# One PSUM bank for sums and values in bursts, three for raw scores, a quarter of them in their own period

## The chip, the cores and the metric

The kernel runs on one core of a Trainium2 chip. The metric is the device time of one execution in microseconds, lower is better. The engines are TensorE (PE in the rows, with PEld for its weight loads), VectorE (DVE), ScalarE (ACT), GpSimd (POOL) and SyncE (SP), which here only issues DMAs.

## What is computed

A small transformer layer over 8 sequences of 384 tokens and 512 features. The first 256 tokens of a sequence come from a state-space convolution (einsum over V = exp(dA_log l)), the other 128 are given. Then, cut to what matters:

```python
h = concatenate([_L0_tok_ref(x, ...), txt], axis=1)
# attention: 16 query heads of 32, 4 key/value heads
scores = einsum('bhqd,bhkd->bhqk', q, k) * HD ** -0.5     # q, k rotated
attn = softmax(scores, axis=-1)
out = einsum('bhqk,bhkd->bhqd', attn, v)
h = h + einsum('bsh,oh->bso', out.reshape(b, s, H), Wo)    # x = layernorm(h) went in
# 64 experts, 6 for each token, at most 64 tokens each, and two shared ones
h = h + ffn(layernorm(h))
```

## The kernel before

The program has three stages: the state-space stage, `attention_phase` (which the change touches alone), and `experts_phase`. The instructions of each engine are written in order by hand, in one loop for each engine, and wait for counts of named semaphores; there is no scheduler. So every engine's queue is strictly in the order of the code.

`attention_phase` runs over periods b = -1 to 7. In period b the softmax and values of sequence b are made, and beside them the next sequence a = b + 1 is prepared (normalised, turned, projected, rotated, heads turned), c = b - 1 is projected out and d = b - 2 is routed to experts. A period has 16 slots n, one for each head; tables such as VALUE_STEPS, Q_SLOT, KV_SLOT and OUT_FIRST give the slot of each piece, and the same tables are read in the loops of all engines.

The pieces that the change and the prediction speak of:

- `scores(b, n)`, L853 to L862: three matmuls into banks 0 to 2, for one head. The operand QT has a row (row 96) with the negated maximum of every query, so that the exponential that follows (ScalarE, L1100) needs no subtraction. Heads 0 and 8 wait for `stacked[0]` and `stacked[1]`: the DMAs that stack the heads (`stack`, L728 and L731) and bring the maxima (`stack_max`, L737), each for half of the heads.
- `raw(a, u)`, L887 to L895, and `row_maximum(a, u)`, L1325 to L1333: unit u of 48 is one bf16 matmul of 128 queries by 384 keys, and VectorE's maximum over its row. Units 0 to 23 are heads 0 to 7, units 24 to 47 heads 8 to 15. Two banks (5 and 6) take turns, and all 48 units of the next sequence stand in slots 8 to 15, six a slot. `max_row` (L1335 to L1341) transposes the maxima of a half into `mrow`, in slots 11 and 15.
- `values(G, q)`, L864 to L885: for group G of four heads, six steps of four matmuls (each a quarter of the array's columns). Steps 0 to 2 sum the exponentials into bank 4, steps 3 to 5 multiply them with the values into bank 3. In four slots the steps are (0, 1), (2, 3), (4), (5). `invert_sums` (L1343) transposes and inverts the sums on VectorE, `divide` (L1354) multiplies.
- `turn_x` and `turn_heads` (L897, L922): transposes of the next sequence's input and of its rotated heads, in slots 0 and 7. ScalarE copies each turned head (L1206), VectorE makes its low part (`q_lo`, L1323), ScalarE converts it for the raw scores (`bf16_heads`).
- `statistics2` and `slots` on VectorE: second layer norm of d (slot 0, L1370 to L1376) and the slots of the experts (slot 1, L1418 to L1422); `routing` in slots 4 to 6 (L1382 to L1413).
- SP's order in a period: `stack(1)`, `stack_max(1)`, the rows of the next but one sequence, rows of the residual, `store_turned`, `store_rows`, `stack(0)`, `stack_max(0)`, `store_sums`.

The wait that guards the turned heads on ScalarE, in slot 7, is not touched by the change:

```python
if i == 0 and a >= 1:
    act.wait_ge(stacked[1], STACK * a)
```

STACK counts the twelve DMAs of `stack` and the four of `stack_max` of one half, so with a = b + 1 the wait is for all of `stacked[1]` up to period b.

## Time and profile before

| what | us |
|---|---|
| median of 3 runs | 1477.85 (1473.19 to 1486.64) |
| the profiled execution's own time | 1462.84 |
| its span, from the first to the last instruction | 1461.0 |
| mean granted TensorE clock | 0.947 |

The span is what the trace covers; the execution's own time is a little over it. The median of the runs is 15 us above the profiled execution. Attention runs from the first scores, at 201.51 us, and seven periods later head 0 of period 7 starts at 743.05. In rows of the trace a line such as `512.60 1.02 DVE L1294 ... x2 [1.46 <-ACT ...]` gives start, duration, engine, line, what it writes and reads, how many instructions are merged, and in brackets the idle time before it with what ended it. An fp32 matmul counts as two instructions in rows of L880.

### The profile page before, as it was taken

To read this page: it belongs to the slowest core of one execution; us is meant where nothing else is said; L and a number is where in the kernel's file an instruction comes from. 1 tells how busy PE (TensorE), PEld (TensorE's weight loads), DVE (VectorE), ACT (ScalarE), POOL (GpSimd) and SP (SyncE) were. 2 spreads that over 40 slices of the span, in tenths; PEclk is the share of its full clock that TensorE was granted. 3 is DMA by queue.
4 is the path that set the end of the run, shared out by engine and by line. 5 is a ranking of instruction groups with operands and counts; after the bars stand their busy time and mean duration, and the time that the engine had idled before them with its cause. 6 is when DMAs were issued, how large, how long until landed. Compare 5 with 4: busy or idle time off the path is not lost. (4 is left out here: it accounts for less than half of the span.)

```text
span 1461.0 us, 23472 instructions
## 1 busy us (share of the span) xinstructions
PE 1267.7 (87%) x9192; PEld 819.4 (56%) x9192; DVE 759.0 (52%) x1667; ACT 420.8 (29%) x695; POOL 501.3 (34%) x453
## 2 busy tenths in 40 slices
PE   5197578889898999989888879999999999999995
PEld 5196434344546464636444768756666656666662
DVE  6984466757676868676866352323222222232221
ACT  2211223444435354444445421111111111111110
POOL 0000101011203434343467376243444444444345
PEclk9698769999999999999999889999999999999998
DMA  3023141321505152524243384799999999998983
GB/s 114 0 60 94 30 103 41 77 50 43 142 17 146 42 131 63 128 66 107 66 137 118 118 291 74 212 309 300 330 304 302 318 337 329 282 362 290 325 267 44
DMA packets 139829, 239.82 MB, mean 164 GB/s; under 512 B 61112, under 2 KB 81224, under 8 KB 139720
## 3 DMA queue, kind: packets, MB, share of 16 engines
q1 hardware_dynamic: 115880, 214.10, 46.0%
q0 software_dynamic: 23840, 24.23, 9.2%
q8 instruction: 73, 1.20, 0.3%
q14 instruction: 36, 0.29, 0.1%
HBM read 175.59 MB, written 38.90 MB: 147 GB/s over the span
## 5 line engine op out<-in xcount | busy, mean ns | idle before, releaser
L1969 POOL DMA_INDIRECT out_rows<-mo_y,mo_scatter_half x128 | 182.1, 1423 | 244.2 <-DMA out_rows<-mo_y,mo_scatter_half 172.3
L1332 DVE TENSOR_REDUCE at_maxes<-at_ps 128x1 f32<-128x384 f32 x384 | 195.1, 551 | 63.2 <-PE at_ps L894 57.3
L1100 ACT ACTIVATE bulk<-at_ps 128x1152 f32<-128x1152 f32 x128 | 144.5, 1129 | 263.4 <-PE at_ps L861 262.3
L1592 POOL DMA_INDIRECT slot_table<-at_toki,at_si x144 | 143.3, 995 | 105.4 <-DVE at_maxes L1332 76.1
L70 PE MATMUL mo_ps<-arena_view,arena_view 128*117 128x384 f32 (+1 forms) x864 | 168.8, 344 | 1.1 <-PEq L549 1.1
L70 PEld LDWEIGHTS mo_ps<-arena_view,arena_view 128*117 128x117 f32 (+1 forms) x864 | 146.6, 179 | 14.6 <-issue 14.5
L894 PE MATMUL at_ps<-late_view,late_view 128*128 128x384 bf16 x384 | 116.7, 354 | 35.8 <-DVE at_maxes L1332 18.0
L852 PE MATMUL at_ps<-arena_view,arena_view 128*128 128x512 f32 (+1 forms) x576 | 114.8, 350 | 3.8 <-ACT arena_view L1185 2.4
L894 PEld LDWEIGHTS at_ps<-late_view,late_view 128*128 128x128 bf16 x384 | 31.2, 98 | 145.7 <-DVE at_maxes L1332 111.7
L852 PEld LDWEIGHTS at_ps<-arena_view,arena_view 128*128 128x128 f32 x576 | 90.3, 193 | 36.6 <-issue 22.3
L861 PE MATMUL at_ps<-arena_view 97*128 97x384 f32 x384 | 97.6, 363 | 9.2 <-DMA arena_view<-at_mrow 5.1
L1944 DVE SCALAR_TENSOR_TENSOR mo_hm<-mo_sil,mo_wcol,mo_ps 128x352 f32<-128x352 f32 x32 | 18.6, 580 | 155.9 <-ACT mo_sil L1868 155.9
L1564 POOL TENSOR_TENSOR arena_view<-arena_view,arena_view 128x640 f32<-128x640 f32 x24 | 37.3, 1555 | 172.4 <-DVE arena_view L1317 172.3
L852 PE MATMUL at_ps<-late_view,late_view 128*128 128x512 f32 x288 | 92.4, 437 | 4.1 <-POOL late_view L1568 2.5
L1568 POOL TENSOR_TENSOR late_view<-arena_view,late_view 128x384 fp32r<-128x384 f32 x32 | 32.0, 1012 | 171.1 <-ACT late_view L1164 171.1
L485 PE MATMUL ss_psK<-arena_view,bulk 64*64 64x64 f32 x2048 | 61.5, 221 | 30.8 <-DVE bulk L431 30.8
L880 PE MATMUL at_ps<-bulk,at_ones 128*32 128x384 f32 x768 | 86.1, 528 | 0.5 <-DVE at_maxes L1332 0.5
L1814 PE MATMUL mo_ps<-bulk,mo_xgT 128*64 128x352 f32 x512 | 81.0, 470 | 5.0 <-DVE mo_xgT L1937 5.0
L880 PE MATMUL at_ps<-bulk,arena_view 128*32 128x384 f32 x768 | 83.3, 508 | 0.0
L78 PE MATMUL mo_ps<-arena_view,arena_view 117*128 117x512 f32 (+1 forms) x324 | 78.9, 397 | 4.9 <-DVE arena_view L1901 4.9
L861 PEld LDWEIGHTS at_ps<-arena_view 97*128 97x128 f32 x384 | 68.5, 195 | 25.5 <-ACT bulk L1100 8.2
L1814 PE MATMUL mo_ps<-late_view,mo_xgT 128*64 128x352 f32 x512 | 79.3, 462 | 1.7 <-DVE mo_xgT L1937 1.7
(218 smaller groups left out, 1820.5 us busy)
## 6 DMA issues: line engine op xcount, KB each, us to landing
bulk<-in_L_ffn_w_gate SPq DMA_DIRECT2D x32, 704.0 KB, 7.4
bulk<-in_L_ffn_w_up SPq DMA_DIRECT2D x32, 704.0 KB, 8.9
late_view<-in_L_ffn_w_gate SPq DMA_DIRECT2D x32, 704.0 KB, 7.5
late_view<-in_L_ffn_w_up SPq DMA_DIRECT2D x32, 704.0 KB, 9.2
arena_view<-arena_view SPq DMA_DIRECT2D x96, 192.0 KB
late_view<-in_L_ffn_w_down SPq DMA_DIRECT2D x32, 512.0 KB, 6.1
bulk<-in_L_ffn_w_down SPq DMA_DIRECT2D x32, 512.0 KB, 6.4
out_rows<-at_hr SPq DMA_DIRECT2D x8, 768.0 KB, 3.8
```

The source lines that it names most:

```text
L70: m = T.matmul(out, self.gu[:, wa, g, k, self.SO[c]:self.SO[c] + self.SW[c]], self.x2[:, xa, k, :], start=(n == 0), stop=(n == last))
L78: m = T.matmul(out, self.h[0:self.SW[c], xa, c, s * P:(s + 1) * P], self.d[0:self.SW[c], wa, c, :], start=(n == 0), stop=(n == last))
L485: m = T.matmul(psK[half, n % 2, i * STEP:(i + 1) * STEP], Pm[half, k % 2, t, h, :], basis, start=(t == 0), stop=(t == 3))
L852: m = T.matmul(out, xs[:, xa, k, x_cols], ws[:, wa, k, w_cols], start=(n == 0), stop=(n == 3 * KC - 1))
L861: m = T.matmul(ps[:, kt, 0:SEQ], QT[:, NH + h // REP, kt * P:(kt + 1) * P], QT[:, h, :], start=True, stop=True)
L880: m = T.matmul(ps[HD * j:HD * (j + 1), 3 + sums, 0:SEQ], w, PT[:, (REP * G + j) % RING, kt, :], start=(kt == 0), stop=(kt == NT - 1))
L894: T.matmul(ps[:, raw_bank(a, u), 0:SEQ], qb[:, r, s * P:(s + 1) * P], kb[:, g, :], start=True, stop=True).then_inc(raw_scores, 1)
L1100: A.activation(PT[:, N % RING, :, :], ps[:, 0:NT, 0:SEQ], ACT.Exp, scale=float(HD) ** -0.5)\
L1332: V.tensor_reduce(maxes[:, half, s, h:h + 1], ps[:, raw_bank(a, u), 0:SEQ], AX.X, ALU.max, negate=True)\
L1592: G.indirect_dma_start(slot_table, bass.IndirectOffsetOnAxis(ap=si[:, e % 2, m:m + 1], axis=0), toki[:, e % 2, m // TOPK:m // TOPK + 1], N ...
L1814: m = M.matmul(ps[CAP * e:CAP * (e + 1), 1 + g, 0:I], xgT[:, k, CAP * e:CAP * (e + 1)], wgu[j][:, e, g, k, :], start=(k == 0), stop=(k == ...
L1969: G.indirect_dma_start(acc_halves, bass.IndirectOffsetOnAxis(ap=scatter_half[:, half, 2 * p + e:2 * p + e + 1], axis=0), y[:, p % 2, e, co ...
```

## The change

Sums and values of a group now share bank 3. All three steps of the sums stand in the first slot of a group, all three of the values in the third. `invert_sums` moves to the second slot, `divide` to the fourth, and the values wait for the first transpose of the inversion, which reads the sums out of the bank. Bank 4 is free for raw scores: units 0 to 35 of the next sequence (36 units, four or five a slot) rotate over banks 4, 5 and 6 and wait for the maximum three units back; units 36 to 47 are made in their own sequence's period, in slots 0 to 6, all in bank 4, each waiting for the maximum of the unit before. Sequence 0 keeps its old places. `max_row` of the second half moves from slot 15 of the period before to slot 6 of the own one, that of the first half from slot 11 to 13. On SP `stack_max(1)` moves behind `store_turned`, and in the last period the first load of shared rows behind it. GpSimd's scatters wait for maxima scaled to 36.

```diff
-        VALUE_STEPS = {0: (0, 1), 1: (2, 3), 2: (4,), 3: (5,)}
+        VALUE_STEPS = {0: (0, 1, 2), 1: (), 2: (3, 4, 5), 3: ()}
...
+        AHEAD_UNITS = 36
+        RAW_EARLY = {1: 37, 2: 39, 4: 42, 5: 44, 6: 46}
+        RAW_LATE = {0: 36, 1: 38, 2: 40, 3: 41, 4: 43, 5: 45, 6: 47}
+
         def raw_units(b, n):
...
-            if -1 <= b < B - 1 and n >= RAW_FROM and (b >= 0 or n < RAW_FROM + REP):
-                return b + 1, range(PER_SLOT * (n - RAW_FROM), PER_SLOT * (n - RAW_FROM + 1))
+            if b == -1 and RAW_FROM <= n < RAW_FROM + REP:
+                return 0, range(PER_SLOT * (n - RAW_FROM), PER_SLOT * (n - RAW_FROM + 1))
+            if 0 <= b < B - 1 and n >= RAW_FROM:
+                return b + 1, range(AHEAD_UNITS * (n - RAW_FROM) // (NH - RAW_FROM),
+                                    AHEAD_UNITS * (n - RAW_FROM + 1) // (NH - RAW_FROM))
             return b + 1, ()
 
+        def own_units(b, n, when):
+            return (when[n],) if b >= 1 and n in when else ()
+
         def raw_bank(a, u):
-            return (7, 4)[u % 2] if a == 0 and u >= HALF_UNITS else 5 + u % 2
+            if a == 0 and u >= HALF_UNITS:
+                return (7, 4)[u % 2]
+            return 4 + u % 3 if u < AHEAD_UNITS else 4
...
-                    if b > 0:
-                        sp.wait_ge(mrow_ready, 2 * b + 2)
-                        stack_max(1)
...
                     store_turned(d)
+                if b > 0:
+                    sp.wait_ge(mrow_ready, 2 * b + 2)
+                    stack_max(1)
+                if b == B - 1:
+                    for done in stacked:
+                        sp.wait_ge(done, STACK * B)
+                    sp.wait_ge(x2T_stored, 16 * (B - 3))
+                    shared_rows_in(0)
+                if prev2:
                     store_rows(d)
...
                 if q == 0:
                     pe.wait_ge(probs_ready, REP * (G + 1))
-                    wait(pe, divide_step, DIVIDE_STEPS * (G - 1) + 1 if G else 0)
-                    wait(pe, max_ready, 0 if G else UNITS)
+                    wait(pe, o_ready, G)
                 if q == NT:
                     pe.wait_ge(v_copied, NT * (b + 1))
-                    wait(pe, o_ready, G)
+                    pe.wait_ge(divide_step, DIVIDE_STEPS * G + 1)
...
-                wait(pe, max_ready, UNITS * a + u - 1)
+                if u < AHEAD_UNITS and (a > 0 or u < HALF_UNITS):
+                    wait(pe, max_ready, UNITS * a + max(u - 2, 0))
+                else:
+                    wait(pe, max_ready, UNITS * a + (u if a else u - 1))
...
-                    for q in steps[0:1]:
+                    for q in steps:
                         values(G, q)
+                    for u in own_units(b, n, RAW_EARLY):
+                        raw(b, u)
                     if prev2 and n == 4:
                         logits(d)
...
+                    for u in own_units(b, n, RAW_LATE):
+                        raw(b, u)
                     for u in units[4:]:
                         raw(of, u)
...
-                    if n % REP == 0:
-                        divide(NKV * b + n // REP - 2)
+                    if n % REP == 1:
+                        invert_sums(NKV * b + n // REP - 1)
+                    if n % REP == REP - 1:
+                        divide(NKV * b + n // REP - 1)
...
+                    for u in own_units(b, n, RAW_EARLY):
+                        row_maximum(b, u)
                     if prev2:
                         routing(d, n)
                     for u in units[2:4]:
                         row_maximum(of, u)
-                    if n % REP == REP - 2:
-                        invert_sums(NKV * b + n // REP - 1)
+                    for u in own_units(b, n, RAW_LATE):
+                        row_maximum(b, u)
...
-                    if nxt and n in (NH * 3 // 4 - 1, NH - 1) and (a > 0 or n < NH - 1):
-                        max_row(a, (n - RAW_FROM) // REP)
-                    if b == 0 and n == REP - 1:
-                        max_row(0, 1)
+                    if nxt and n == (RAW_FROM + REP - 1 if a == 0 else RAW_FROM + 5):
+                        max_row(a, 0)
+                    if main and n == (REP - 1 if b == 0 else 6):
+                        max_row(b, 1)
```

TensorE at the start of period 4, before. L861 are scores, L904 the turns of the next input (late_view_54 is the identity), L880 the sums (from at_ones) and values, L852 projections, 128x512 for queries and 128x256 for keys and values:

```order
L904 MATMUL at_ps<-late_view_54,arena_view_1714 128x128 x6
L880 MATMUL at_ps<-bulk,at_ones 32x384 x4
L904 MATMUL at_ps<-late_view_54,arena_view_1714 128x128 x6
L880 MATMUL at_ps<-bulk,at_ones 32x384 x4
L861 MATMUL at_ps<-arena_view_1724 128x384 x3
L880 MATMUL at_ps<-bulk,at_ones 32x384 x4
L880 MATMUL at_ps<-bulk,arena_view_1723 32x384 x4
L852 MATMUL at_ps<-arena_view_65,arena_view_1715 128x512 x12
L861 MATMUL at_ps<-arena_view_1724 128x384 x3
L880 MATMUL at_ps<-bulk,arena_view_1723 32x384 x4
L852 MATMUL at_ps<-arena_view_65,arena_view_1715 128x256 x12
```

And after, where the same lines are L875, L920, L893 and L866, and L910 is a raw score:

```order
L920 MATMUL at_ps<-late_view_54,arena_view_1714 128x128 x6
L893 MATMUL at_ps<-bulk,at_ones 32x384 x12
L920 MATMUL at_ps<-late_view_54,arena_view_1714 128x128 x6
L910 MATMUL at_ps<-late_view_1722,late_view_1721 128x384
L875 MATMUL at_ps<-arena_view_1724 128x384 x3
L910 MATMUL at_ps<-late_view_1722,late_view_1721 128x384
L866 MATMUL at_ps<-arena_view_65,arena_view_1715 128x512 x12
L910 MATMUL at_ps<-late_view_1722,late_view_1721 128x384
L875 MATMUL at_ps<-arena_view_1724 128x384 x3
L893 MATMUL at_ps<-bulk,arena_view_1723 32x384 x12
L910 MATMUL at_ps<-late_view_1722,late_view_1721 128x384
L866 MATMUL at_ps<-arena_view_65,arena_view_1715 128x256 x12
```

The sums are one burst between the turns, the values one burst in slot 2, and a raw score of the own sequence stands on either side of the first projection.

VectorE in the same place, before: L1294 makes the low parts of the input, L1365 adds the residual, L1370 to L1376 are the second statistics, L1418 to L1422 the slots of the experts:

```order
L1294 TENSOR_TENSOR arena_view_1715<-at_ps,arena_view_1715 128x384 x4
L1365 TENSOR_TENSOR at_hr<-at_hr,at_ps 128x512
L1370 BN_STATS at_bn<-at_hr 128x6 x3
L1373 BN_AGGR at_mv<-at_bn 128x2 x3
L1375 TENSOR_SCALAR at_shift<-at_mv 128x3
L1376 TENSOR_SCALAR at_ve<-at_mv 128x3
L1418 TENSOR_REDUCE at_sf<-at_hv 128x18
L1420 CAST at_si<-at_sf 128x18
L1421 CAST at_toki<-at_tokf 128x3
L1422 TENSOR_SCALAR at_tokf<-at_tokf 128x3
```

After, with L1350 a row maximum and L1367 to L1369 the inversion of the sums:

```order
L1312 TENSOR_TENSOR arena_view_1715<-at_ps,arena_view_1715 128x384 x4
L1383 TENSOR_TENSOR at_hr<-at_hr,at_ps 128x512
L1388 BN_STATS at_bn<-at_hr 128x6 x3
L1391 BN_AGGR at_mv<-at_bn 128x2 x3
L1393 TENSOR_SCALAR at_shift<-at_mv 128x3
L1394 TENSOR_SCALAR at_ve<-at_mv 128x3
L1350 TENSOR_REDUCE at_maxes<-at_ps 128x1
L1367 STREAM_TRANSPOSE arena_view_1725<-at_ps 128x384
L1368 RECIPROCAL at_rcol<-arena_view_1725 128x12
L1369 STREAM_TRANSPOSE arena_view_1725<-at_rcol 128x384
L1436 TENSOR_REDUCE at_sf<-at_hv 128x18
```

The maximum of unit 36 stands behind the second statistics, and the inversion between it and the expert slots; two more maxima follow those.

VectorE in slots 6 and 7 of period 4, before: L1403 to L1413 are the routing, L1323 the low parts of the heads, L1332 the first maxima of the next sequence:

```order
L1403 RECIPROCAL at_rsum<-at_ssum 128x3
L1405 TENSOR_SCALAR late_view_1727<-late_view_1728,at_rsum 128x64 x3
L1411 TENSOR_TENSOR late_view_1728<-at_ps,at_base 128x192
L1412 TENSOR_SCALAR at_lg<-late_view_1728 128x192
L1413 TENSOR_TENSOR at_base<-at_base,at_ps 128x64
L1349 STREAM_TRANSPOSE arena_view_1725<-at_ps 128x384
L1350 RECIPROCAL at_rcol<-arena_view_1725 128x12
L1351 STREAM_TRANSPOSE arena_view_1725<-at_rcol 128x384
L1323 TENSOR_TENSOR arena_view_1720<-at_ps,arena_view_1719 128x384 x5
L1332 TENSOR_REDUCE at_maxes<-at_ps 128x1 x2
```

And after:

```order
L1350 TENSOR_REDUCE at_maxes<-at_ps 128x1
L1421 RECIPROCAL at_rsum<-at_ssum 128x3
L1423 TENSOR_SCALAR late_view_1727<-late_view_1728,at_rsum 128x64 x3
L1429 TENSOR_TENSOR late_view_1728<-at_ps,at_base 128x192
L1430 TENSOR_SCALAR at_lg<-late_view_1728 128x192
L1431 TENSOR_TENSOR at_base<-at_base,at_ps 128x64
L1350 TENSOR_REDUCE at_maxes<-at_ps 128x1
L1358 STREAM_TRANSPOSE at_mrow<-at_maxes 128x96
L1377 TENSOR_TENSOR arena_view_1726<-at_ps,arena_view_1725 128x384
L1341 TENSOR_TENSOR arena_view_1720<-at_ps,arena_view_1719 128x384 x5
L1350 TENSOR_REDUCE at_maxes<-at_ps 128x1 x6
```

A maximum stands before the routing and one behind it, the transpose of the maxima (L1358) follows, then a division in place of the inversion, and then the low parts.

## Rows read from the trace of the kernel before

**Rows 1.** Stretches: length, busy us (count) of PE, PEld, DVE, ACT, POOL; clock, DMA share
```profile
201.51:278.75 77.24, 64.33 (x364) 33.59 (x364) 53.10 (x119) 28.46 (x39) 5.68 (x5) 0.90 0.26 57
...
510.27:552.60 42.33, 38.06 (x269) 25.30 (x267) 29.75 (x82) 23.50 (x44) 15.41 (x17) 0.96 0.49 131
552.60:587.85 35.25, 33.21 (x201) 15.50 (x202) 28.93 (x59) 11.96 (x14) 16.71 (x18) 1.00 0.21 44
...
743.05:771.72 28.67, 21.75 (x167) 10.80 (x165) 16.19 (x46) 17.36 (x29) 19.66 (x21) 0.91 0.79 236
```

**Rows 2.** Groups by line, 552.60 to 587.85: busy us, mean ns, idle before
```profile
L1332 DVE TENSOR_REDUCE at_maxes<-at_ps 128x1 f32<-128x384 f32 x48 | 24.4, 551 | 6.3 <-PE at_ps L894 4.7 <-issue 1.3
...
L894 PE MATMUL at_ps<-late_view,late_view 128*128 128x384 bf16 x48 | 13.6, 333 | 2.5 <-DVE at_maxes L1332 1.4 <-issue 0.5
L852 PE MATMUL at_ps<-late_view,late_view 128*128 128x512 f32 x36 | 11.8, 437 | 0.0
```

**Rows 3.** Timeline of TensorE, period 4, and two steps of sums in period 7
```profile
510.27 0.69 PE L861 MATMUL at_ps<-arena_view 97*128 97x384 f32 x3
...
514.94 0.79 PE L861 MATMUL at_ps<-arena_view 97*128 97x384 f32 x3
...
517.09 3.06 PE L852 MATMUL at_ps<-arena_view,arena_view 128*128 128x512 f32 x12
519.99 0.69 PE L861 MATMUL at_ps<-arena_view 97*128 97x384 f32 x3
...
526.27 0.77 PE L861 MATMUL at_ps<-arena_view 97*128 97x384 f32 x3
...
530.32 0.77 PE L861 MATMUL at_ps<-arena_view 97*128 97x384 f32 x3
...
538.26 0.69 PE L861 MATMUL at_ps<-arena_view 97*128 97x384 f32 x3
...
541.83 0.69 PE L861 MATMUL at_ps<-arena_view 97*128 97x384 f32 x3
...
544.44 0.77 PE L861 MATMUL at_ps<-arena_view 97*128 97x384 f32 x3
...
552.60 0.48 PE L894 MATMUL at_ps<-late_view,late_view 128*128 128x384 bf16 x2 [0.51 <-issue]
...
743.67 1.50 PE L880 MATMUL at_ps<-bulk,at_ones 128*32 128x384 f32 x16
745.10 0.79 PE L861 MATMUL at_ps<-arena_view 97*128 97x384 f32 x3
```

**Rows 4.** Timeline of VectorE, first half of period 4
```profile
515.97 1.88 DVE L1370 BATCH_NORM_STATS2 at_bn<-at_hr 128x6 f32<-128x512 f32 x3
...
518.38 1.34 DVE L1418 TENSOR_REDUCE at_sf<-at_hv 128x18 f32<-128x1152 f32 x1
...
522.50 0.57 DVE L1349 STREAM_TRANSPOSE arena_view<-at_ps 128x384 f32<-128x384 f32 x1
...
534.25 1.88 DVE L1282 BATCH_NORM_STATS2 at_bn<-arena_view 128x6 f32<-128x512 f32 x3 [5.20 <-DMA arena_view<-in_txt]
...
541.06 1.97 DVE L1391 TENSOR_TENSOR at_hot<-at_iota,at_mf 128x384 bf16<-128x384 f32 x3
...
547.30 0.21 DVE L1413 TENSOR_TENSOR at_base<-at_base,at_ps 128x64 f32<-128x64 f32 x1
```

**Rows 5.** Timeline of ScalarE, slot 7 of period 4: first and last copies of turned heads
```profile
546.91 0.87 ACT L1206 ACTIVATE arena_view<-at_ps 128x384 fp32r<-128x384 f32 x2 [0.47 <-PE at_ps L931]
...
551.41 0.49 ACT L1206 ACTIVATE arena_view<-at_ps 128x384 fp32r<-128x384 f32 x1
```

**Rows 6.** Timeline of all engines ahead of period 0: a row of maxima on its way
```profile
197.03 0.28 DVE L1340 STREAM_TRANSPOSE at_mrow<-at_maxes 128x96 f32<-128x96 f32 x1
197.34 3.01 SPq L737 DMA_DIRECT2D arena_view<-at_mrow  x4
...
201.51 1.33 PE L861 MATMUL at_ps<-arena_view 97*128 97x384 f32 x3 [5.11 <-DMA arena_view<-at_mrow]
```

20 lines of the change are left out of this document (7 added, 13 removed).

## The prediction

> **What bounds the kernel now.** The page tells that TensorE and VectorE are both well filled while attention runs, but not which of them sets the pace, so I read the stretches by stage next. In the first half of period 4 (from the scores of head 0, at 510.27, to the first raw score of the next sequence, at 552.60: 42.33 us) TensorE is busy for 38.06 us and VectorE for 29.75; in the second half (35.25 us) they are busy for 33.21 and 28.93 [rows 1]. Then the groups of the second half: VectorE spends 24.4 us on the 48 row maxima and idles 6.3 before them, mostly for the raw scores; TensorE idles 2.5 before the raw matmuls [rows 2]. So the second half is a ping-pong over two banks in which either engine is nearly full. The first half, read in the timelines, is one chain through both engines [rows 3, 4], and it ends with the turned heads: ScalarE copies five of them, VectorE makes the low parts, and only then can the first raw score start [rows 5]. Neither half has much room, so what is added to a chain is likely to show.
>
> **The change, part by part.** Times from here on count from 510.27, in period 4; slot n is the work around head n.
>
> Second half. 36 of the 48 raw scores stay, over three banks. VectorE loses 12 maxima of 0.51 us each (24.4 / 48): 6.1 us. TensorE: two steps of sums in succession take 1.43 us (743.67 to 745.10) [rows 3], so a burst of three is 2.1 and four bursts are 8.4. The eight scores are about 0.55 each, 4.4; the 36 raw scores about 0.2 each, 7.2; the output projection keeps its 36 matmuls, 11.8 us of busy time [rows 2], of which some 10 count beside the overlap of one with the next. That is 30.0. In slots 9, 11 and 13 VectorE (five maxima and an inversion of 1.4 us, or a division and a residual) has 1.0 to 1.3 us more to do than TensorE, and three banks hide only a part. I take 2.3 us of waits: 32.3, against 35.25, a gain of 3 a period. Its ends are 0 (the bursts win nothing) and 6.1 (all the maxima removed count).
>
> First half, slots 0 and 1. Now scores 1 start at 4.67 and the first query projection at 6.82 [rows 3]. With three steps of sums between the turned inputs, scores 1 start near 4.5. But the maximum of unit 36, issued in slot 0, stands on VectorE behind the second statistics, which run from 5.70 to 8.1 [rows 4], and 0.4 later in the new order: it ends at 9.0. Unit 37 writes the same bank 4 and waits for it, and the projection stands behind unit 37: it starts at 9.3 and ends at 12.2. Unit 38 waits for maximum 37, which stands behind the inversion (1.45 us, from 12.23 now) and the slot sums (2.85 us, from 8.11 now) [rows 4]: 9.0 + 1.45 + 2.85 + 0.5 = 13.8. So scores 2 start at 14.2, where they start at 9.72 now.
>
> Slots 2 to 7, by how long each lasts now between scores [rows 3]. Slot 2: 6.28, plus 1.3 (a burst for one step) and 0.4 (two raw scores): 7.95, scores 3 at 22.1. Slot 3: 4.05; a step of values goes, but it covered a wait for the copied values, so 4.2, scores 4 at 26.3. Slot 4: 7.94, plus 0.7 (three steps for two) and two raw scores, 8.8: scores 5 at 35.1. Slot 5: 3.57, minus two steps, plus two raw scores, plus 1.6 for maximum 44, which stands behind inversion and rope (together 2.7): scores 6 at 39.2. Slot 6: 2.61, plus 1.3, plus the wait of unit 46 for maximum 45, behind the one-hot work (3.0 us, from 30.8 now [rows 4]): scores 7 at 43.7. VectorE then has the routing of slot 6 (3.0 us, ending at 37.2 now), maximum 47 and the transpose of the maxima. The row of maxima is ready at 47.3.
>
> The landing. Four small DMAs carry that row into the operand of the scores. They are issued in slot 2 now, long before scores 8 want them. At the one place where the scores wait for such DMAs, the transpose ends at 197.31, the four issues take 3.01 us and the scores start at 201.51, 4.2 us later [rows 6]. So the row lands at 51.5. ScalarE's first copy of a turned head (L1206) has a wait for stacked[1] that counts all periods so far, and it now waits for exactly this landing. From that copy to the first raw score are 5.69 us (546.91 to 552.60) [rows 3, 5], nearly all of it ScalarE's own work; I take 5.5. First raw score at 57.0, against 42.33: +14.7. With the second half's -3, a full period is 11.7 longer. The Trainium skill ("DMA: Bandwidth & Descriptors", section Rules for kernel authors) says to issue a DMA early and wait for it late, so that its fixed cost is overlapped, and the change does the opposite. This trace agrees, with the 1.2 us from the end of the last issue to the scores [rows 6].
>
> Bounds of the first half. If every new wait in slots 1, 5 and 6 were covered, the 12 raw scores (2.4) and the landing behind a row ready at about 40 would be left: near +7. If each wait is a third longer than I have it, +18.
>
> Other edits. No exponential, projection or scatter is added. GpSimd's scatter thresholds follow the 36 units; its queue waits for the maxima, not they for it. The next rows are issued 2.9 us earlier on SP, which takes away VectorE's wait of 5.20 before the statistics at 23.98 [rows 4]; in the chain above the statistics start at 27.0, so this wins nothing more. The shared bank 3 lets values wait for the first transpose of the inversion, issued a slot earlier: nothing, or 0.8 once at the end of the stage.
>
> **The sum.** Periods 3 to 5: 3 x 11.7 = 35. Period 6: 12. Period 2 has no slot sums, so unit 38 waits less: 10.5. Period 1 has neither second statistics nor routing; its row of maxima is ready at 36.5 by the same steps, and the landing makes it +9.4 - 3 = 6.4. Period 0 (77.24 us [rows 1]) keeps its first half, and in its second VectorE loses the 6.1 with little else to do: -6.5. The fill before it has three banks: -1. Period 7 has short slots, and its scores 8 start 28.67 after its head 0 now [rows 1]; stalls and landing put them near 40, and I take +10. Together 35 + 12 + 10.5 + 6.4 - 6.5 - 1 + 10 = 66.4. The profiled execution took 1462.84 by its own time, so 1529; the median of the runs shown, 1477.85, is 15 us above that execution, and I set the sum on it: 1544, say 1545.
>
> **Rivals.** First, the kernel gains. In the second half the ping-pong over two banks is what bounds, and the 6.1 us of maxima removed count in full, 43 us over seven periods, while the twelve moved ones fall into VectorE's idle time of the first half (42.33 - 29.75 = 12.6 us [rows 1]). For it: that idle time is twice what they need. Against it: queues run in order, and the second statistics lie just between two units of one bank. It decides at the row of maxima: ready by 37 after the period's start, it lands before ScalarE asks; later than that it delays. With half of the 43 kept it gives -20, 1458.
>
> Second, only the landing counts. Units 37, 38, 44 and 46 wait less than I found, the first half grows by 8, and the second shrinks by 4: 6 x 4 + 10 - 6.5 - 1 = 26.5, 1504. For it: TensorE idles 4.3 us of the first half now, and new waits may lie in the old ones' place.
>
> Third, the clock on top. It is granted at 0.96 in the first half of period 4 and at 1.00 in the second; in period 7's short slots, where TensorE is busy 21.75 of 28.67 us, it is 0.91 [rows 1]. With waits of 4 us in slot 1 and 7 around slot 8, a mean lower by 0.03 to 0.05 over a first half of 57 us would cost 1.7 to 2.9 us, 12 to 20 over seven periods: 1557 to 1565. "TensorE: Matmul & The Clock Gate" of the Trainium skill (section Why this matters for your kernels) warns of idle gaps between bursts of matmuls; by that rule my error would lie on this side.
>
> **How the numbers follow.** The chain as worked out gets 0.60, the landing alone 0.15, the clock on top 0.15, the gain 0.10, part of which ends near zero. A change of 1% is about what a measurement of this kernel can tell from none. So faster by over 1% gets 0.07, within 1% 0.07, slower by over 1% 0.86. The range goes from 1500 (the landing alone, a little less) to 1572 (the clock, with waits somewhat longer than I have them). The likeliest case alone would be 1525 to 1562.
>
> **What would show it.** Right: ScalarE's copy of the first turned head idle until the landing of DMAs from at_mrow in periods 1 to 6; TensorE waiting about 4 us in slot 1 for a row maximum; first halves of 55 to 59 us and second halves of 30 to 34. Wrong: first halves under 46 us, the row of maxima ready within 40 us of the period's start, or second halves still of 35. A granted clock under 0.92 in the first halves would speak for the third rival.

## The result

The changed kernel took 1559.13 us (median of 4 runs, 1553.81 to 1566.12), the kernel before beside it on the same chip 1477.16 (4 runs, 1473.19 to 1486.64). The ratio is 1.0548, with a 95% interval of [1.0482, 1.0613]: slower by 82 us. The forecast was 1545, slower by 67, in a range of 1500 to 1572.

The profiled execution of the changed kernel took 1566.12, 7 above its median, that of the kernel before 1462.84, 14 below its own. So the two traces lie 103 us apart, not 82. Up to head 15 of period 7 the difference is 88 (starts at 883.2 and 795.1). The other 15 us lie behind it, where the change moves only one thing, the first load of shared rows; that load was not tested by itself. The same stretch takes 662 to 683 us in the traces of all the kernels below (666 before, 681 changed), so I read nothing from it.

First the stretches of the changed kernel, in the columns of [rows 1]: the first half of period 4 (534.35 is its head 0), the second half, and period 7 up to head 8.

```profile
534.35:591.23 56.88, 41.24 (x280) 28.97 (x279) 33.70 (x95) 23.71 (x44) 16.26 (x18) 0.87 0.36 98
591.23:626.92 35.69, 32.24 (x189) 16.66 (x190) 21.90 (x47) 11.49 (x14) 15.82 (x17) 0.91 0.21 44
...
811.02:858.20 47.18, 27.84 (x178) 14.26 (x176) 24.63 (x63) 18.23 (x29) 26.98 (x28) 0.73 0.48 144
```

The first half grew by 14.6 us (42.33 before), while TensorE is busy only 3.2 more: most of it is waits. The second half did not shrink (35.25 before) though VectorE has 7 us less to do in it. Period 7 needs 47.18 to reach head 8, where it took 28.67. The granted clock fell in all three, from 0.96, 1.00 and 0.91 to 0.87, 0.91 and 0.73.

The groups of the second half, columns as in [rows 2], now with 36 units:

```profile
L1350 DVE TENSOR_REDUCE at_maxes<-at_ps 128x1 f32<-128x384 f32 x36 | 17.8, 550 | 13.8 <-PE at_ps L910 7.9 <-remote 5.8
...
L910 PE MATMUL at_ps<-late_view,late_view 128*128 128x384 bf16 x36 | 11.2, 354 | 4.6 <-issue 1.8 <-DVE at_maxes L1350 1.8
L866 PE MATMUL at_ps<-late_view,late_view 128*128 128x512 f32 x36 | 11.2, 441 | 0.7 <-DVE at_hr L1383 0.7
```

What VectorE gained by twelve maxima (24.4 to 17.8) went into idle time before the others (6.3 to 13.8), mostly for raw scores. TensorE idles more too, 4.6 for 2.5. Neither is the one that is full.

### The profile page after: what moved, and what is told of

Read it like the earlier page. It is cut to its first block and busy times, and to the rows that moved or that the text cites. A ratio compares the mean times of both kernels' runs of the same rounds, so it can differ in the third digit from the quotient of the medians.

```text
span 1564.3 us, 23475 instructions
## 1 busy us (share of the span) xinstructions
PE 1280.9 (82%) x9192; PEld 855.4 (55%) x9192; DVE 740.7 (47%) x1667; ACT 420.4 (27%) x695; POOL 501.4 (32%) x453
## 5 line engine op out<-in xcount | busy, mean ns | idle before, releaser
L1350 DVE TENSOR_REDUCE at_maxes<-at_ps 128x1 f32<-128x384 f32 x384 | 195.2, 551 | 184.7 <-PE at_ps L910 166.9
L910 PE MATMUL at_ps<-late_view,late_view 128*128 128x384 bf16 x384 | 124.0, 363 | 84.0 <-DVE at_maxes L1350 60.2
L70 PEld LDWEIGHTS mo_ps<-arena_view,arena_view 128*117 128x117 f32 (+1 forms) x864 | 146.5, 179 | 14.6 <-issue 14.5
L910 PEld LDWEIGHTS at_ps<-late_view,late_view 128*128 128x128 bf16 x384 | 33.7, 100 | 183.4 <-DVE at_maxes L1350 107.7
L866 PE MATMUL at_ps<-arena_view,arena_view 128*128 128x512 f32 (+1 forms) x576 | 125.5, 372 | 9.3 <-ACT arena_view L1203 7.8
L875 PE MATMUL at_ps<-arena_view 97*128 97x384 f32 x384 | 108.3, 394 | 12.7 <-DMA arena_view<-at_mrow 11.4
L866 PEld LDWEIGHTS at_ps<-arena_view,arena_view 128*128 128x128 f32 x576 | 98.6, 206 | 26.2 <-DVE arena_view L1335 9.8
L866 PE MATMUL at_ps<-late_view,late_view 128*128 128x512 f32 x288 | 85.1, 428 | 9.5 <-DVE at_hr L1383 4.9
L875 PEld LDWEIGHTS at_ps<-arena_view 97*128 97x128 f32 x384 | 75.6, 210 | 21.1 <-DMA arena_view<-at_mrow 12.1
L893 PE MATMUL at_ps<-bulk,at_ones 128*32 128x384 f32 x768 | 84.2, 581 | 0.3 <-ACT bulk L1118 0.3
L485 PEld LDWEIGHTS ss_psK<-arena_view,bulk 64*64 64x64 f32 x2048 | 62.4, 139 | 32.5 <-issue 32.5
```

The lines of the kernel that those rows point to most:

```text
L70: m = T.matmul(out, self.gu[:, wa, g, k, self.SO[c]:self.SO[c] + self.SW[c]], self.x2[:, xa, k, :], start=(n == 0), stop=(n == last))
L485: m = T.matmul(psK[half, n % 2, i * STEP:(i + 1) * STEP], Pm[half, k % 2, t, h, :], basis, start=(t == 0), stop=(t == 3))
L866: m = T.matmul(out, xs[:, xa, k, x_cols], ws[:, wa, k, w_cols], start=(n == 0), stop=(n == 3 * KC - 1))
L875: m = T.matmul(ps[:, kt, 0:SEQ], QT[:, NH + h // REP, kt * P:(kt + 1) * P], QT[:, h, :], start=True, stop=True)
L893: m = T.matmul(ps[HD * j:HD * (j + 1), 3, 0:SEQ], w, PT[:, (REP * G + j) % RING, kt, :], start=(kt == 0), stop=(kt == NT - 1))
L910: T.matmul(ps[:, raw_bank(a, u), 0:SEQ], qb[:, r, s * P:(s + 1) * P], kb[:, g, :], start=True, stop=True).then_inc(raw_scores, 1)
```

## The chain of waits in the trace

TensorE in slots 0 to 2 of period 4, and then around head 8:

```profile
534.36 0.69 PE L875 MATMUL at_ps<-arena_view 97*128 97x384 f32 x3
...
538.63 0.82 PE L875 MATMUL at_ps<-arena_view 97*128 97x384 f32 x3
543.67 0.50 PE L910 MATMUL at_ps<-late_view,late_view 128*128 128x384 bf16 x1 [4.21 <-DVE at_maxes L1350]
543.76 5.52 PE L866 MATMUL at_ps<-arena_view,arena_view 128*128 128x512 f32 x12
549.09 0.54 PE L910 MATMUL at_ps<-late_view,late_view 128*128 128x384 bf16 x1
549.18 1.07 PE L875 MATMUL at_ps<-arena_view 97*128 97x384 f32 x3
...
591.23 0.80 PE L910 MATMUL at_ps<-late_view,late_view 128*128 128x384 bf16 x2 [1.82 <-issue]
591.96 3.16 PE L893 MATMUL at_ps<-bulk,at_ones 128*32 128x384 f32 x24
...
600.12 2.14 PE L893 MATMUL at_ps<-bulk,arena_view 128*32 128x384 f32 x24
```

VectorE at the same start:

```profile
540.65 1.88 DVE L1388 BATCH_NORM_STATS2 at_bn<-at_hr 128x6 f32<-128x512 f32 x3
...
543.06 0.55 DVE L1350 TENSOR_REDUCE at_maxes<-at_ps 128x1 f32<-128x384 f32 x1
...
545.01 1.35 DVE L1436 TENSOR_REDUCE at_sf<-at_hv 128x18 f32<-128x1152 f32 x1
...
546.99 0.56 DVE L1350 TENSOR_REDUCE at_maxes<-at_ps 128x1 f32<-128x384 f32 x1
```

Unit 36 was made before 538.63, but its maximum stands behind the second statistics and starts at 543.06. So unit 37 waits 4.21 us for it, and the query projection with it. Maximum 37 stands in the same way behind inversion and expert slots (546.99). But it is done at 547.55, and unit 38 starts at 549.09: what holds unit 38 is the projection, which runs at half clock and takes 5.52 us.

The row of maxima at the end of the first half, on SP and on ScalarE:

```profile
581.61 2.96 SPq L748 DMA_DIRECT2D arena_view<-at_mrow  x4
```

```profile
585.77 0.87 ACT L1224 ACTIVATE arena_view<-at_ps 128x384 fp32r<-128x384 f32 x2 [5.49 <-DMA arena_view<-at_mrow]
```

ScalarE had nothing else to do and waited 5.49 us, until 4.16 after the first issue. In [rows 5] the same copy starts without such a wait. ScalarE waits six times for these DMAs in the whole trace, 30.7 us together, once in each of periods 1 to 6; it doesn't wait for them at all in the kernel before. What TensorE waited for in the first half of period 4 (us in all, times, longest) are these two above all, the maxima and, at 586.91, the turned heads behind the landing:

```profile
PE at_ps L910 <- DVE at_maxes L1350: 6.3, 4, 4.2
PE at_ps L947 <- DVE arena_view L1341: 5.7, 1, 5.7
```

## The experiments

Each kernel was made from the kernel before or from the changed one. The ratio is to the kernel before as it ran beside each of them; its median there was 1474 to 1483, so the ratios compare a little better than the medians. Beside the ratio, the table gives the means of periods 3 to 5 in the profiled execution, in us: first half (head 0 to the first raw score of the next sequence), second half, time at half clock (1.2 GHz), and, for period 7, head 0 to head 8. A profiled execution can lie 14 us from its median, so differences below 2 us a period are not to be read alone.

| kernel | median | ratio to before | first | second | half clock | to head 8, period 7 |
|---|---|---|---|---|---|---|
| before | 1477.16 | 1 | 42.4 | 36.1 | 4.6 | 28.7 |
| changed | 1559.13 | 1.0548 | 56.7 | 35.3 | 20.5 | 47.2 |
| e1, bursts, shared bank, 3 raw banks | 1515.34 | 1.0254 | 45.4 | 39.0 | 10.2 | 30.2 |
| e2, the same with 2 raw banks | 1536.60 | 1.0411 | 44.7 | 43.0 | 10.2 | 34.2 |
| e10, bursts alone | 1530.29 | 1.0391 | 44.6 | 42.2 | 13.7 | 28.2 |
| e3, changed, landing split off | 1531.36 | 1.0358 | 51.5 | 34.5 | 12.5 | 48.6 |
| e4, changed, maxima 36, 37 first | 1531.60 | 1.0356 | 53.2 | 34.8 | 12.5 | 44.6 |
| e5, changed, added matmuls | 1543.87 | 1.0483 | 56.5 | 33.3 | 8.0 | 47.6 |
| e9, e3 to e5 together | 1494.62 | 1.0144 | 50.6 | 31.7 | 0 | 40.2 |
| e6, e1 with added matmuls | 1497.90 | 1.0163 | 44.4 | 37.7 | 1.1 | 34.2 |
| e7, before with added matmuls | 1473.78 | 0.9959 | 42.7 | 35.3 | 2.3 | 29.1 |
| e8, spread steps, shared bank, 3 raw banks | 1495.62 | 1.0136 | 46.3 | 35.8 | 6.8 | 35.2 |
| e11, e8 with early inversion | 1474.28 | 0.9985 | 45.6 | 36.4 | 8.0 | 28.3 |
| e12, e11 with added matmuls | 1474.79 | 0.9951 | 44.5 | 35.2 | 0 | 34.2 |

### e1 and e2: the bursts and the banks without the moved units

Both are the kernel before with this (cut to the main lines), all 48 raw scores staying ahead:

```diff
-VALUE_STEPS = {0: (0, 1), 1: (2, 3), 2: (4,), 3: (5,)}
+VALUE_STEPS = {0: (0, 1, 2), 1: (), 2: (3, 4, 5), 3: ()}
...
-ps[HD * j:HD * (j + 1), 3 + sums, 0:SEQ]
+ps[HD * j:HD * (j + 1), 3, 0:SEQ]
...
                 if q == NT:
                     pe.wait_ge(v_copied, NT * (b + 1))
-                    wait(pe, o_ready, G)
+                    pe.wait_ge(divide_step, DIVIDE_STEPS * G + 1)
...
-                    if n % REP == 0:
-                        divide(NKV * b + n // REP - 2)
+                    if n % REP == 1:
+                        invert_sums(NKV * b + n // REP - 1)
+                    if n % REP == REP - 1:
+                        divide(NKV * b + n // REP - 1)
```

e1 has besides:

```diff
-            return (7, 4)[u % 2] if a == 0 and u >= HALF_UNITS else 5 + u % 2
+            return (7, 4)[u % 2] if a == 0 and u >= HALF_UNITS else 4 + u % 3
```

and each raw score of it waits for the maximum three units back instead of two.

> The kernel before with the bursts, the shared bank 3 and raw scores over three banks, but all 48 raw scores ahead, as before. If the moved raw scores and the late landing of the maxima are the whole of the loss, this is no slower than before: 2 to 3 us a period are won in the second half (33 to 34 us from the first raw score instead of 35 to 37) and the inversion out of slot 6 takes about 1 us off the first half, 1455 to 1468 against a median of 1477. If the bursts themselves cost (values and sums in one bank, each waiting for VectorE), it is 1490 or more.

> The kernel before with the bursts and the shared bank 3 alone; the raw scores keep two banks. If the third bank is what helps the second half, this lies 12 to 20 us above the one with three banks, at 1472 to 1485, since slots without values now have four to six raw scores in succession over two banks. If the bursts help by themselves, it lies within 5 us of the one with three banks.

Measured: e1 1515.34, ratio 1.0254 [1.0173, 1.0335]; e2 1536.60, 1.0411 [1.0338, 1.0485]. So this half of the change, which I had as a help, costs 40 us by itself, and 61 without the third raw bank. The third bank is worth 21, all of it in the second half (43.0 to 39.0). That is about half of the 82, and it was in none of my cases. Costs that are measured alone need not add up in the changed kernel, though: there the second half has only 36 raw scores.

### e10: the bursts alone

e2 with the banks of the kernel before:

```diff
-ps[HD * j:HD * (j + 1), 3, 0:SEQ]
+ps[HD * j:HD * (j + 1), 3 + sums, 0:SEQ]
...
                 if q == NT:
                     pe.wait_ge(v_copied, NT * (b + 1))
-                    pe.wait_ge(divide_step, DIVIDE_STEPS * G + 1)
+                    wait(pe, o_ready, G)
```

> The kernel before with the bursts alone: all sums of a group in its first slot into bank 4, all values in its third into bank 3, inversion in the second slot and division in the fourth, two raw banks and all 48 units ahead. It differs from the kernel with bursts, shared bank and two raw banks (1536.6, +61 over before) in the sharing only. If it is the sharing (sums wait for the division, values for the inversion) that costs, this runs at 1480 to 1500. If it is the bursts (twelve matmuls in one slot, none in the next), it stays at 1520 to 1540.

Measured: 1530.29, 1.0391 [1.0327, 1.0456], the same as e2 within the intervals. It is the bursts; with them the shared bank costs nothing that can be told. What they do is in the trace. TensorE of e10 at the start of the second half of period 4:

```profile
584.24 0.80 PE L894 MATMUL at_ps<-late_view,late_view 128*128 128x384 bf16 x2 [1.12 <-issue]
584.97 4.07 PE L880 MATMUL at_ps<-bulk,at_ones 128*32 128x384 f32 x24
588.97 0.51 PE L894 MATMUL at_ps<-late_view,late_view 128*128 128x384 bf16 x2
589.97 0.80 PE L894 MATMUL at_ps<-late_view,late_view 128*128 128x384 bf16 x2 [0.49 <-DVE at_maxes L1330]
...
592.13 0.80 PE L894 MATMUL at_ps<-late_view,late_view 128*128 128x384 bf16 x2 [0.37 <-DVE at_maxes L1330]
...
594.55 0.80 PE L894 MATMUL at_ps<-late_view,late_view 128*128 128x384 bf16 x2 [0.82 <-DVE at_maxes L1330]
```

and VectorE beside it:

```profile
584.75 1.02 DVE L1330 TENSOR_REDUCE at_maxes<-at_ps 128x1 f32<-128x384 f32 x2 [0.61 <-PE at_ps L894]
589.35 3.18 DVE L1330 TENSOR_REDUCE at_maxes<-at_ps 128x1 f32<-128x384 f32 x6 [3.57 <-PE at_ps L894]
```

Two raw scores fill the two banks, then the burst runs for 4.07 us, and VectorE is through with both maxima after 1.02 and idles 3.57. Behind the burst the raw scores come without anything between them, and TensorE waits for maxima, three times in this piece. In the kernel before one step (0.85 us) stands between two pairs of raw scores, about as long as the two maxima need. Over the second half the groups of e10 read:

```profile
L1330 DVE TENSOR_REDUCE at_maxes<-at_ps 128x1 f32<-128x384 f32 x48 | 24.4, 553 | 13.9 <-PE at_ps L894 13.5
...
L894 PE MATMUL at_ps<-late_view,late_view 128*128 128x384 bf16 x48 | 15.0, 350 | 7.8 <-DVE at_maxes L1330 5.3 <-issue 1.1
```

VectorE idles 7.6 more than in [rows 2] and TensorE 5.3 more, with the same work: both wait in turn. A part is the clock: this burst ran at half of it, and a full period has 13.7 us of half clock for 4.6. How much of the 56 us that is was not tested in this kernel; e6 below tests it in e1.

### e3: the landing split off

The changed kernel, with semaphores of their own for the maxima, on which the scores wait but ScalarE's head copy does not:

```diff
-... mrow[HD * j:HD * j + NH // 2, half, :, :]).then_inc(stacked[half], 16)
+... mrow[HD * j:HD * j + NH // 2, half, :, :]).then_inc(maxed[half], 16)
...
                     pe.wait_ge(stacked[2 * h // NH], STACK * (b + 1))
+                    pe.wait_ge(maxed[2 * h // NH], MAXED * (b + 1))
```

`max_row` on VectorE also waits for the earlier `maxed` only, no longer for the stacked heads.

> The changed kernel, with the four DMAs of the maxima on semaphores of their own, so that ScalarE's copy of the turned heads waits for the stacked heads alone and only the scores wait for the maxima. My theory: the copies start near 46 us of a full period instead of 51.4, scores 8 still wait for the landing at 51.4, and the first raw score comes near 52 instead of 56.9. Six periods of 4 to 5 us: about 28 us less than the changed kernel, near 1531. The rival, that the granted clock carries the loss behind slot 8: under 10 us less, with the same half-clock time of 20 us a period.

Measured: 1531.36, 1.0358 [1.0287, 1.0429], 28 less than the changed kernel. ScalarE starts the copies of period 4 at once (head 0 stands at 520.0):

```profile
564.35 1.13 ACT L1122 ACTIVATE bulk<-at_ps 128x1152 f32<-128x1152 f32 x1 [1.17 <-PE at_ps L879]
565.38 0.87 ACT L1228 ACTIVATE arena_view<-at_ps 128x384 fp32r<-128x384 f32 x2
...
572.37 1.13 ACT L1122 ACTIVATE bulk<-at_ps 128x1152 f32<-128x1152 f32 x1 [2.33 <-PE at_ps L879]
```

That is 45.4 after head 0, where the changed kernel had 51.4. The second half shrank a little too, with less half clock (12.5 for 20.5), so a part of the 28 is clock. Period 7, where no head is turned, gained nothing: 48.6 to head 8, for 47.2.

### e4: maxima 36 and 37 first

The changed kernel, on VectorE alone (the two maxima go from their old places in slots 0 and 1):

```diff
+                    if b >= 1 and n == 0:
+                        row_maximum(b, RAW_LATE[0])
+                        row_maximum(b, RAW_EARLY[1])
                     if prev2 and n == 0:
                         residual(d, NT - 1)
                         statistics2(d)
```

> The changed kernel, with the maxima of units 36 and 37 ahead of the residual and the second statistics on VectorE. My theory of queue order: unit 37 and the query projection behind it no longer wait for the statistics, scores 2 come near 9 to 10 us of a period instead of 14.8, unit 39 then waits some 2 us for maximum 38 behind the expert slots, scores 3 come near 19.2 instead of 22.9, and the row of maxima 3 to 4 us earlier: about 20 us less than the changed kernel, near 1538. If the row of maxima is bound by VectorE's work in slots 4 to 6 rather than by this wait, scores 3 move and the landing doesn't: within 5 us of the changed kernel.

Measured: 1531.60, 1.0356 [1.0265, 1.0447], also 28 less. TensorE, with head 0 at 527.3:

```profile
533.52 0.34 PE L910 MATMUL at_ps<-late_view,late_view 128*128 128x384 bf16 x1 [1.09 <-DVE at_maxes L1350]
533.62 3.01 PE L866 MATMUL at_ps<-arena_view,arena_view 128*128 128x512 f32 x12
...
536.51 0.82 PE L875 MATMUL at_ps<-arena_view 97*128 97x384 f32 x3
538.21 2.14 PE L893 MATMUL at_ps<-bulk,arena_view 128*32 128x384 f32 x24 [0.88 <-DVE arena_view L1367]
541.57 0.34 PE L910 MATMUL at_ps<-late_view,late_view 128*128 128x384 bf16 x1 [1.22 <-DVE at_maxes L1350]
```

The wait of 4.21 is 1.09 now, and the projection behind it takes 3.01 instead of 5.52. Scores 2 start 5.6 earlier, at 9.2 after head 0, but two new waits stand in slot 2: the values for the inversion (0.88) and unit 39 for maximum 38 (1.22). Of the 5.6, the first half kept 3.5. Here too a part is clock: 2.5 us of the 5.6 are the projection, which no longer runs at half clock behind the long wait.

### e5, e6 and e7: the clock

All three add matmuls whose result is not read, into a bank that is free there, where TensorE waits in slots 6 to 8: 30 a period in the changed kernel (e5), 18 in e1 (e6), 6 in the kernel before (e7). e5's core (two more stand in slot 6):

```diff
+            def fill(bank, count):
+                for _ in range(count):
+                    T.matmul(ps[:, bank, :], WxT[:, 0, 0, 0:P], WxT[:, 0, 0, 0:512], start=True, stop=True)
...
+                    if main and nxt and n == 8:
+                        fill(4, 6)
...
+                    if main and nxt and n == 7:
+                        pe.wait_ge(probs_ready, NH * b + 8)
+                        fill(0, 22)
```

> The changed kernel with 30 more fp32r matmuls of 512 columns a period, whose results nobody reads, placed where TensorE waits anyway: 2 before the places in slot 6, 22 before the last two turned heads in slot 7 (TensorE idles 5.7 us there), 6 behind scores 8. They show what the low clock costs, since no wait is taken away. If the clock falls because TensorE waits for the landing, the half-clock time of a full period goes from 20 us to 10 or less, slot 8 from 7.2 us to about 5.5, and the kernel is 10 to 20 us faster than the changed one although it computes more. If the clock doesn't matter, it is unchanged or up to 8 us slower.

> Bursts and three banks with all 48 raw scores ahead, plus 18 such idle matmuls a period: 10 before the places in slot 6 (2.5 us of waiting there), 2 in slot 7, 6 behind scores 8. Theory: with the values out of slots 5 and 7, TensorE has nothing to do while VectorE makes the mask and the low parts, its clock falls, and the first burst then takes 3.9 us instead of 2.1. So half-clock time should go from 10 us a period to under 4, slot 8 from 8.2 to 5 to 6, and the time to 1490 to 1500. The rival, that the bursts cost by the order of the raw scores and their maxima: the half-clock time falls, but the kernel stays at 1510 or above.

> The kernel before with 6 idle matmuls a period in slots 6 and 7. It has 3.4 us of half clock a period, of which the raw scores of slot 8 pay a part: up to 1.5 us a period, so 1466 to 1477 against 1476. No change if its clock falls for other reasons.

Measured: e5 1543.87, 1.0483 [1.0400, 1.0566]; e6 1497.90, 1.0163 [1.0098, 1.0228]; e7 1473.78 (10 runs), 0.9959 [0.9917, 1.0001]. By the medians that is 15 us in the changed kernel and 17 in e1, by the ratios 10 and 13, and in the traces head 15 of period 7 comes 9 and 13 us earlier. The intervals of each pair overlap, so the size is not sharp: 10 to 15 us and 13 to 17 are the clock. In the kernel before it is nothing that can be told. e5's stretches of period 4, head 0 at 529.10:

```profile
529.10:585.70 56.60, 46.82 (x310) 33.13 (x309) 33.69 (x95) 23.69 (x44) 16.28 (x18) 0.94 0.36 98
585.70:618.70 33.00, 29.32 (x189) 15.73 (x190) 21.85 (x46) 11.52 (x14) 15.76 (x17) 1.00 0.22 47
```

The first half is as long as in the changed kernel, since the half clock in slot 1, behind the long wait, is still there (the added matmuls stand later). The second half runs at 2.4 GHz throughout (1.00) and is 2.7 shorter. The first burst in it takes 2.14 us instead of 3.16:

```profile
586.14 2.14 PE L897 MATMUL at_ps<-bulk,at_ones 128*32 128x384 f32 x24
```

The Trainium skill ("TensorE: Matmul & The Clock Gate", section HAM oscillation) counts the penalty as half of the throttled time. By that rule, as an estimate, the 81 us less at half clock over the whole trace (281 in the changed kernel, 200 in e5) would be 40 us. The run shows 10 to 15. A likely reason, not tested, is that much of that time TensorE was waiting anyway.

### e9: the three cures together

The edits of e3, e4 and e5 in one kernel.

> The changed kernel with a semaphore of its own for the landing of the maxima, with maxima 36 and 37 ahead of the second statistics, and with 30 matmuls a period whose result is not read in the waits around slots 6 to 8. Alone these gave -28, -28 and -15 us. If they cure three different waits, most of it adds up: 1485 to 1500. If ScalarE's head copy, once freed from the landing, waits for the last maxima or the scores of head 8 instead, or if the matmuls only help where a wait is long, the cures overlap and it stays at 1505 to 1520. The bursts with the shared bank, which alone cost 38 us over the kernel before, stay in; by either theory it stays slower than before.

Measured: 1494.62, 1.0144 [1.0097, 1.0191]. The three alone gave 28, 28 and 15, together 71 (by the ratios 28, 28 and 10, together 66); here 64.5 are gone (60 by the ratio). So they are in the main three different losses; in the main only, because e3 and e4 had each taken some half clock away too. What e9 still has over the kernel before, at full clock, is in its stretches of period 4:

```profile
516.60:567.20 50.60, 43.85 (x310) 31.64 (x308) 33.50 (x95) 23.94 (x45) 15.99 (x18) 1.00 0.41 110
567.20:598.90 31.70, 28.70 (x190) 15.52 (x190) 22.05 (x46) 11.29 (x14) 16.09 (x17) 1.00 0.22 49
```

In the means, bursts and moved quarter together cost 8.2 in the first half (50.6 against 42.4) and bring 4.4 in the second (31.7 against 36.1). In the first half of period 4 TensorE still waits four times for maxima, 3.9 us in all.

### e8, e11 and e12: the shared bank without bursts

e8 is e1 with the steps spread over the four slots of a group again, but in the shared bank; inversion and division stay in the second and fourth slot, at their ends:

```diff
-VALUE_STEPS = {0: (0, 1, 2), 1: (), 2: (3, 4, 5), 3: ()}
+VALUE_STEPS = {0: (0, 1), 1: (2,), 2: (3, 4), 3: (5,)}
```

> Shared bank 3 and three banks for all 48 raw scores, as in the run with bursts, but the steps spread again: (0, 1), (2), (3, 4), (5) in the four slots of a group, with the inversion at the end of the second slot and the division at the end of the fourth. If it is the bursts and the gaps they leave that cost, this has the first half of before (40 to 42 us), a second half of 33 to 35 and about 3.4 us of half clock a period: 1455 to 1480. If it is the shared bank itself, with its wait of the values for the inversion, it stays at 1500 or above.

Measured: 1495.62, 1.0136 [1.0055, 1.0217]: 20 less than e1, but 16 over the kernel before, in between the two expectations. Its second half is that of the kernel before (35.8), so the bursts' part is gone. In the first, slot 2 takes 10.5 us where it took 6.3:

```profile
513.99 0.69 PE L861 MATMUL at_ps<-arena_view 97*128 97x384 f32 x3
516.61 2.13 PE L879 MATMUL at_ps<-bulk,arena_view 128*32 128x384 f32 x16 [1.94 <-DVE arena_view L1351]
518.67 2.61 PE L852 MATMUL at_ps<-arena_view,arena_view 128*128 128x256 f32 x12
```

The values wait 1.94 for the inversion to read the sums out of the bank, and what follows runs partly at half clock. That inversion (L1351) stood on VectorE behind the expert slots. e11 moves it ahead of them, and in the other groups ahead of the third raw maximum:

```diff
+                    if n == 1:
+                        invert_sums(NKV * b - 1)
                     if prev3 and n == 1:
                         slots(e)
```

> The spread steps over a shared bank and three raw banks (1495.6), with VectorE's inversion moved up in its slot, ahead of the expert slots in slot 1 and ahead of the third raw maximum elsewhere. If what is left there is the wait of the values for the inversion in the shared bank (slot 2: 10.5 us against 6.3 before, slot 14: 7.0 against 4.7), slot 2 falls to 7 to 8 and the time to 1470 to 1482. If VectorE's stall for the sums takes the place of TensorE's wait, nothing changes: 1490 to 1500.

Measured: 1474.28 (10 runs), 0.9985 [0.9961, 1.0009], 21 less than e8 and equal to the kernel before. In slot 2 the wait is gone, and values and projection take 1.50 and 1.69 for 2.13 and 2.61:

```profile
520.07 0.68 PE L861 MATMUL at_ps<-arena_view 97*128 97x384 f32 x3
520.68 1.50 PE L879 MATMUL at_ps<-bulk,arena_view 128*32 128x384 f32 x16
522.11 1.69 PE L852 MATMUL at_ps<-arena_view,arena_view 128*128 128x256 f32 x12
...
545.77 1.51 PE L879 MATMUL at_ps<-bulk,arena_view 128*32 128x384 f32 x8 [2.87 <-DVE arena_view L1351]
```

But the last row shows that the wait for the inversion is not gone everywhere: in slot 6 the values wait 2.87 us for it, where they waited 1.94 in e8. So in period 4 slot 2 is 3.2 us shorter than in e8 and slot 6 is 2.5 longer, and the first half is as good as unchanged (46.1 for 46.4). Over periods 0 to 6 the two traces differ by only 1.4 us. e11's trace is 14 us shorter, by 9 us in period 7 up to head 15 and 6 behind it. So slot 2 does not account for the 21 us of the medians, and what does is not shown.

Nothing is won against the kernel before either. e11's second half is 36.4 and that of the kernel before 36.1, so between spread steps a third raw bank brings nothing that shows there. Its first half is 3.2 longer (45.6 for 42.4); periods 0 and 1 are 3.4 and 1.2 shorter in its trace. Which of its edits does which was not tested. e12 adds 18 matmuls whose result is not read, as in e6, ten of them ahead of the values in slot 6.

> The kernel with spread steps, shared bank, three raw banks and the early inversion (1474.3, equal to the kernel before), with 18 matmuls a period whose result is not read: 10 ahead of the values in slot 6, 2 in slot 7, 6 in slot 8. Its trace has 3 to 10 us of half clock in most periods, around slots 5 to 9. In the kernel with bursts the same matmuls gave 17 us (1515.3 to 1497.9), in the kernel before nothing that could be told (0.996). If the half clock is what is left there, 1460 to 1467, faster than both kernels. If the matmuls only take the place of waits that the values and places have anyway, and delay what follows, 1472 to 1480.

Measured: 1474.79 (12 runs; the kernel before beside it, 17 runs, 1483.15), 0.9951 [0.9915, 0.9987]. No half clock is left in periods 1 to 6, but the gain is half a per cent, no more than e7 has without any of the change. It was the second expectation that held. No version here beats the kernel before by an amount worth having.

## Why the prediction was right, and where it was not

**The chain of the first half held.** From period 4's head 0, predicted and measured: unit 37 at 9.3 and 9.3; scores 2 at 14.2 and 14.8, scores 3 at 22.1 and 22.9, scores 4 at 26.3 and 27.2, scores 5 at 35.1 and 35.6, scores 6 at 39.2 and 39.9, scores 7 at 43.7 and 43.9; issue of the row of maxima at 47.3 and 47.3; ScalarE's copy at 51.5 and 51.4; first raw score at 57.0 and 56.9. The orders of the engines with durations of the trace before were enough. One of these agreements is luck. Scores 2 were to come at 14.2 because unit 38 waits for maximum 37 until 13.8. The slot sums ahead of that maximum took 1.98 us, not 2.85, it was done at 13.2, and it held nothing. The query projection ran at half clock instead, ended at 14.9 and not at 12.2, and held unit 38 until 14.7. One sum in the chain is also 0.2 too small as written (slot 4: 7.94 + 0.7 + 0.4 is 9.0, not 8.8; measured 8.5).

**The landing** was found where it was expected, on ScalarE in periods 1 to 6. e3 shows its price, 28 us, and e4 that of VectorE's order in slots 0 and 1, 28 us, each with some clock in it. The Trainium skill's rule of the early issue and late wait ("DMA: Bandwidth & Descriptors", section Rules for kernel authors) is borne out by e3: the issue is as late there, and taking the wait to where the data is used gave back 28.

**The periods.** Predicted -6.5, +6.4, +10.5, three times +11.7, +12; in the traces -5.7, +6.8, +10.9, +12.7, +15.0, +12.9, +15.9. The first three hold within 1. The other four are 9.4 us too small together. Up to head 15 of period 7 the traces lie 88 us apart, where the sum had 66: besides those 9.4, period 7 up to head 8 is 8.5 short, and the rest are small terms. The medians lie 82 apart, and that is part of why 1545 came as near to 1559 as it did.

**The second half was mis-sized.** The term was "32.3, against 35.25, a gain of 3 a period"; it measured 35.7 in period 4 and 35.3 in the mean of periods 3 to 5 (36.1 before), a gain of 0.8 at best. "Second halves still of 35" was one of my own signs of being wrong, and it came. The step that failed is the clock: 32.3 was worked out from matmuls at full clock. Where the matmuls of e5 and e9 held it at 2.4 GHz, the half took 33.3 and 31.7. In the changed kernel TensorE had waited for the landing through slots 7 and 8, and the first burst then ran at half clock.

**Period 7** was put at +10 and measured +18.5. The waits of TensorE there for maxima and for the landing, up to head 8:

```profile
PE at_ps L910 <- DVE at_maxes L1350: 8.8, 5, 3.6
PE at_ps L875 <- DMA arena_view<-at_mrow: 6.1, 1, 6.1
```

Those are 14.9 us (in all, times, longest), where the forecast had about 10 for everything. TensorE idles 12.4 more than before up to head 8 (19.3 for 6.9) and is busy 6.1 more (27.84 for 21.75), with twelve raw scores more and a clock of 0.73 instead of 0.91. Two of the four bursts in that stretch show the clock:

```profile
821.29 4.07 PE L893 MATMUL at_ps<-bulk,arena_view 128*32 128x384 f32 x24
...
834.74 2.95 PE L893 MATMUL at_ps<-bulk,at_ones 128*32 128x384 f32 x24
```

**The rivals.** The gain fell: the row of maxima was ready at 47, not by 37. The landing alone fell: the first half grew by 14.3, not by 8. The clock on top, 1557 to 1565 with a chance of 0.15, fits best: 1559, and its sign was a granted clock under 0.92 in the first halves; it was 0.87. Its place was in part another. It was costed in the first halves, and what e5 gave back, it gave in the second ones. In slot 1 the half clock made the projection 2.5 us longer, of which at most 1.5 can have delayed unit 38 (14.7 for 13.2). I had put its chance too low. I knew the new waits and that the clock was at 0.91 where slots are short; a forecast that adds 10 us of waits to a period should have had a lower clock in its likeliest case.

**What no case had** is that the bursts themselves lose. The prediction costed them by their work (2.1 us, twelve matmuls) and asked what they free, not what they cover. e10 shows +56 for them alone. In the changed kernel less of that is seen. My reading is that VectorE has twelve maxima fewer in the same half, so that the moved units pay for the bursts; no run has the moved units without them. By e1 and e2 the third raw bank gives back 21 of 61, and e6 says that 13 to 17 of e1's 40 are clock. That my sum came near is luck in this respect: its 2.3 us of waits in the second half stood for something of the kind without its name. The edit costed at "nothing", the values' wait for the inversion, was right for the bursts (e2 against e10). With spread steps the place of the inversion was worth 21 (e8 against e11).

**Left open.** Spread steps with the moved quarter and early maxima were not tried together, so what the moved units would bring without bursts is not measured; nor were spread steps in a shared bank with two raw banks, or e10 at full clock. Nor is it shown why head 8 of period 7 comes at 34 to 35 in e2, e6, e8 and e12 and at 28 to 30 in e1, e10 and e11.

## What to carry to other kernels

Before pieces of one engine's work are gathered into a burst, look at what each of them stands beside: here a step of 0.85 us between two raw scores was about as long as the two maxima it covered, and gathering three of them made both engines wait in turn, in part at half clock. A buffer that this frees may only repair what the gathering broke; try the buffer with the old order too. And when a wait is moved to an in-order queue, read what stands behind it there that needs neither the data nor the wait: a counter of its own for the late transfer gave back 28 us.

## What was not expected of the hardware

A burst of twelve matmuls of a quarter of the columns (x24 in its rows) takes 2.14 us at full clock and up to 4.07 at half, so a wait of TensorE ahead of it can be paid twice. Eighteen to thirty added matmuls a period, which do nothing, made two kernels 10 to 17 us faster, but the kernel before, which had 155 us of half clock in its whole trace, gained at most 0.8% by six of them, and e12 lost all half clock in six periods for half a per cent.
